# Gate and up projections of a feed-forward as seven-product block products

## The reference

```python
    Wg = dequant_nvfp4(gate_W_packed, gate_scales)   # (4096, 512)
    Wu = dequant_nvfp4(up_W_packed, up_scales)       # (4096, 512)
    Wd = dequant_nvfp4(down_W_packed, down_scales)   # (512, 4096)
    gate = jnp.einsum('th,nh->tn', xt, Wg)
    up = jnp.einsum('th,nh->tn', xt, Wu)
    gelu = jnp.tanh(0.7978845608028654 * (gate + 0.044715 * gate ** 3)) * gate * 0.5 + gate * 0.5
    inter = gelu * up
    out = jnp.einsum('tn,hn->th', inter, Wd)
    ...
x = x + _L0_ffn_ref(_layernorm(x, axis=-1), ...)
```

## Time and profile before

| what | us |
|---|---|
| median of 3 runs (1642.74 to 1647.78) | 1646.12 |
| the profiled execution's own time | 1646.68 |
| its span, first to last instruction | 1644.9 |
| TensorE busy in the span | 1526.4 (93%) |
| VectorE busy | 893.8 (54%) |
| ScalarE busy | 560.6 (34%) |
| GpSimd busy | 123.2 (7%) |

### The profile page before, as it was taken

How to read it: one execution, slowest core, us unless ns; L and a number is a source line. 1 busy time by engine, 2 the same in 40 slices (tenths; PEclk the granted TensorE clock), 3 DMA queues, 4 the chain that set the end, 5 groups by cost and what they waited for, 6 DMA issues and landing times.

```text
span 1644.9 us, 29227 instructions
## 1 busy us (share of the span) xinstructions
PE 1526.4 (93%) x9280; PEld 769.8 (47%) x9280; DVE 893.8 (54%) x2152; ACT 560.6 (34%) x1323; POOL 123.2 (7%) x189
## 2 busy tenths in 40 slices
PE   5887987897899788999999999999999999999998
PEld 3355445544554554444444444444444444444443
DVE  7488468567855976555434534534534544444222
ACT  4378148526833862221212222221222222222111
POOL 1512002100200352000000000000000000000000
PEclk8979989998999999999999999999999999999999
DMA  6641432142125221212112112112112111111111
GB/s 192 163 141 52 122 92 66 59 128 89 60 65 155 88 86 38 81 41 80 40 40 80 40 40 79 41 40 75 45 40 72 48 40 65 54 40 43 59 51 51
DMA packets 73553, 118.41 MB, mean 72 GB/s; under 512 B 10096, under 2 KB 54384, under 8 KB 68848
## 3 DMA queue, kind: packets, MB, share of 16 engines
q1 hardware_dynamic: 73456, 117.20, 22.7%
HBM read 93.32 MB, written 23.86 MB: 71 GB/s over the span
## 4 chain that ended last, share of the span: by engine, by line
PE 79%; DVE 10%; issue 6%; DMA 2%; SPq 1%; ACT 1%; DVEq 0%; ACTq 0%
PE bank L534 23%; PE bank L536 23%; PE bank L535 23%; DVE bank L1135 3%; PE bank L591 3%; PE bank L610 2%; PE bank L547 1%; DVE mx L1135 1%; PE bank L580 1%; DMA qk_dram<-qk 1%; DVE w_split L1328 1%; PE bank L619 1%; DVE prob_t L1149 1%; DVE nmx L1142 1%; PE bank L664 1%
## 5 line engine op out<-in xcount | busy, mean ns | idle before, releaser
L534 PE MATMUL bank<-xf,ring 128*128 128x512 f16 x1024 | 388.1, 379 | 0.0
L535 PE MATMUL bank<-xf,ring 128*128 128x512 f16 x1024 | 388.1, 379 | 0.0
L536 PE MATMUL bank<-xf,ring 128*128 128x512 f16 x1024 | 388.1, 379 | 0.0
L1258 DVE SCALAR_TENSOR_TENSOR inter<-bank,col,gel 128x512 f32<-128x512 f32 x128 | 96.0, 750 | 377.9 <-PE bank L536 377.6
L534 PE MATMUL bank<-ring,hid 128*128 (+1 forms) x512 | 194.1, 379 | 4.2 <-DVE o_t L1122 1.8
L964 ACT CAST hid<-inter 128x512 f16<-128x512 f32 x128 | 79.3, 619 | 347.8 <-DVE inter L1258 331.9
L535 PE MATMUL bank<-ring,hid 128*128 (+1 forms) x512 | 194.0, 379 | 0.0
L536 PE MATMUL bank<-ring,hid 128*128 (+1 forms) x512 | 194.0, 379 | 0.0
L960 ACT ACTIVATE gel<-bank,col 128x512 f32<-128x512 f32 x128 | 88.0, 688 | 300.5 <-PE bank L536 300.5
L591 PE MATMUL bank<-ident,prob 128*128 128x128 f32 x640 | 122.4, 299 | 44.4 <-DVE prob_t L1149 37.8
L1135 DVE CUSTOM_DVE_ANT_0 bank<-bank,mask,col 128x128 f32<-128x128 f32 (+3 forms) x256 | 142.5, 557 | 38.3 <-PE bank L580 24.5
(11 more groups left out here) (141 smaller groups left out, 1820.0 us busy)
## 6 DMA issues: line engine op xcount, KB each, us to landing
xf<-xf_dram SPq DMA_DIRECT2D x32, 1024.0 KB, 4.9
stack<-qk_dram SPq DMA_DIRECT2D x128, 128.0 KB, 3.2
sc_in<-scale_t SPq DMA_DIRECT2D x32, 384.0 KB
qk_dram<-qk SPq DMA_DIRECT2D x32, 256.0 KB, 3.1
packed_t<-pk_t SPq DMA_DIRECT2D x32, 192.0 KB, 2.0
pk_in<-packed_t SPq DMA_DIRECT2D x32, 192.0 KB
X<-in_x_dram SPq DMA_DIRECT2D x4, 1024.0 KB, 6.9
pk_in<-L_ffn_gate_W_packed_dram SPq DMA_DIRECT2D x16, 256.0 KB, 2.9
```

What stands on the lines that cost most here:

```text
L534: pe.matmul(o, lhs(0), rhs(0), start=first, stop=False)
L535: pe.matmul(o, lhs(0), rhs(1), start=False, stop=False)
L536: return pe.matmul(o, lhs(1), rhs(0), start=False, stop=stop)
L1258: nc.vector.scalar_tensor_tensor(inter[:, q], bank[2 * q + 1][:], C_I, gel[:, q], ALU.mult, ALU.mult).then_inc(int_out, 1)
```

## The change

The four batches are taken as two pairs. For a pair, the activations are a two by two block matrix: its two contraction blocks are the two nibbles' rows (each of two tiles of 128), its two column blocks the two batches (512 columns each). The weights of a block of 256 hidden rows are a two by two block matrix too: two blocks of 128 hidden rows by the same two contraction blocks. Their product, eight block products before, is made from seven block products of sums of blocks (Strassen's, in Winograd's form). It is done for gate (x = 0) and for up (x = 1).

- TensorE: `product` makes one of seven block products, two contraction tiles by three matmuls, into banks 0 to 3; three of the seven are added onto what a bank holds. `group` runs the new order: for each pair of batches, two blocks of 256 hidden rows (q = 0, 1) with 2 x 7 products each, and then `down` for the two batches, 48 matmuls each. This is called a pass below: 168 + 96 matmuls, 16 passes. The first block of a pass is q = 0.
- VectorE: `first_sums` and `corners`, four sums of a bank and an SBUF tile for each of gate and up; `inner`, the product of gelu and up, from SBUF but for one; `hidden_tail`.
- ScalarE: `copy_x`, `copy_z`, two copies out of a bank for each of gate and up; `gelu`; `hidden_head`; `heads`, the heads of the weights in three or four pieces.
- GpSimd: `corner`, one sum for each of gate and up, and `weight_sum`, four sums of weight blocks per half block. Heads and tails are now made of the weights' sums too.
- The sums of activation blocks are made once for each pair (`operand_part`, 13 steps for each of two halves, one half on VectorE and one on GpSimd), and both pairs stay in SBUF. The loads of xf at each iteration go.
- In the attention of the last batch GpSimd does more of the first blocks' weights (`weights_beside`). The output is stored tile by tile.

```diff
+        PRODUCTS = ((A11, B11, 0), (S2, T2, 1), (S3, T3, 3), (S1, T1, 2), (A12, B21, 0), (A22, T4, 3), (S4, B22, 2))
...
+            if step in (5, 8, 11, 12):
+                eng.wait_ge(t_hi[h], 4 * pair + (5, 8, 11, 12).index(step) + 1)
+            out, in0, in1, op = ((t1, x(B12, 0), x(B11, 0), ALU.subtract), (t1, t1, x(B12, 1), ALU.add), (t1, t1, x(B11, 1), ALU.subtract),
...
+            ops.tensor_tensor(out, in0, in1, op).then_inc(t_step[h], 1)
...
-            def mlp_loads(i2, odd, dequant, nxt):
...
+            for d in range(2 * NB - B, 2 * NB):
+                b = d % B
+                for t in range(TT):
+                    sp.wait_ge(acc_out, TT * d + t + 1)
+                    sp.dma_start(out[b, P * t:P * t + P, :], X[:, b * TT + t, :]).then_inc(out_stored, 16)
...
+            def corner(m, x):
+
+                pool.wait_ge(comb, 8 * m + 4 * x + 2)
+                pool.wait_ge(c_copied, 4 * m + 2 * x + 2)
+                nc.gpsimd.tensor_tensor(c22[x][:], c22[x][:], m5[x][:], ALU.add).then_inc(c22_out, 1)
...
+            def closing():
+                for step in range(4, T_STEPS):
+                    operand_part(pool, nc.gpsimd, 0, 1, step)
+                for which in (0, 1, 2, 3):
+                    tail(0, 1, which)
+                corner(0, 0)
...
-            def gate_up(it, par, s):
...
+                elif which == IN_C11:
+                    pe.wait_ge(c_copied, 4 * m + 2 * x + 1)
+                elif which == IN_C21:
+                    pe.wait_ge(comb, 8 * m + 4 * x + 2)
...
+                for h in range(2):
+                    mm = three(bank[at][:], lambda a: G[slot][:, op_w, a, 2 * x + h, :], lambda a: xs[pair][:, op_x, a, h, :],
+                               h == 0 and which < IN_C11, h == 1, which >= IN_C11)
+                mm.then_inc(prod, 1)
...
+            def gate_up(m, w, q, weights):
+                copy_x(m, 0)
+                copy_z(m, 0)
+                gelu(m, 0)
+                gelu(m, 1)
+                gelu(m, 2)
+                copy_x(m, 1)
+                gelu(m, 3)
+                copy_z(m, 1)
+                for idx in range(4):
+                    hidden_head(m, w, q, idx)
+                if weights is not None:
+                    heads(*weights)
...
+            def first_sums(m, x):
+
+                dve.wait_ge(prod, product_done(m, x, IN_Y))
+                dve.wait_ge(c_copied, 4 * m + 2 * x + 1)
+                nc.vector.tensor_tensor(c12[x][:], bank[1][:], c21[x][:], ALU.add).then_inc(comb, 1)
...
+            def hidden(m, q):
+                inner(m, 0)
+                corners(m, 1)
+                hidden_tail(m, q, 0)
+                inner(m, 1)
+                inner(m, 2)
+                hidden_tail(m, q, 1)
+                inner(m, 3)
+                hidden_tail(m, q, 2)
+                hidden_tail(m, q, 3)
...
+            def gate_up(m, q, early, weights, late):
+
+                first_sums(m, 0)
+                if early is not None:
+                    tails(*early)
+                if weights is not None:
+                    unpack(*weights, range(0, 3))
+                corners(m, 0)
+                if weights is not None:
+                    unpack(*weights, range(3, 6))
+                first_sums(m, 1)
+                if weights is not None:
+                    scaled(*weights)
+                hidden(m, q)
+                if late is not None:
+                    tails(*late)
...
+            def closing(n):
+                for step in range(T_STEPS):
+                    operand_part(dve, nc.vector, 0, 0, step)
+                residual(n, wo_full, 4, C_O, x1_done)
+                norm_beside(1, n, 0, True)
```

More of the change, by code:

```diff
@@ new lines, in weight_sums, with head, tail @@
+            def weight_sums(nb, half):
+                for which in range(4):
+                    weight_sum(nb, half, which)
+            def head(nb, half, which):
+                weights_whole(pool, nb, half, which)
+                dst, src = piece(nb % 3, half, which, 0)
+                nc.gpsimd.tensor_copy(dst, src).then_inc(dq_hi, 1)
+            def tail(nb, half, which, ops=None):
+                pool.wait_ge(dq_hi, 7 * nb + 3 * half + which + 1)
+                (lo, full), hi = piece(nb % 3, half, which, 1), piece(nb % 3, half, which, 0)[0]
+                if ops is not None:
+                    lo, full, hi = lo[:, ops], full[:, ops], hi[:, ops]
+                ins = nc.gpsimd.tensor_tensor(lo, full, hi, ALU.subtract)
+                done = low_sem(half, which)
+                if done is not None and (ops is None or ops.stop == 4):
@@ new lines, in products, with down @@
+            def products(m, x, which, pair, slot, nb):
+                for one in which:
+                    product(m, x, one, pair, slot, nb)
+            def down(w, pair, beta, slots, nbs):
+                d = 2 * w + beta
+                first = isinstance(d, int) and d == 0
+                if first:
+                    pe.wait_ge(spread_lo[2], B * KT)
+                pe.wait_ge(wd_lo, nbs[0] + 1)
+                pe.wait_ge(hid_lo, 8 * w + 2 * beta + 2)
+                for r in range(2):
+                    for t in range(TT):
+                        if r == 0 and not first:
+                            pe.wait_ge(acc_out, 4 * d + (t - 3))
+                        three(bank[4 + t][:], lambda a: hid[:, beta, 0, r, a, P * t:P * t + P], lambda a: Wd[slots[0]][:, a, r, :], r == 0, False)
+                pe.wait_ge(wd_lo, nbs[1] + 1)
+                pe.wait_ge(hid_lo, 8 * w + 2 * beta + 6)
+                for t in range(TT):
+                    for r in range(2):
+                        mm = three(bank[4 + t][:], lambda a: hid[:, beta, 1, r, a, P * t:P * t + P], lambda a: Wd[slots[1]][:, a, r, :], False, r == 1)
+                    mm.then_inc(down_done, 1)
```

736 lines of the change are left out of this document (473 added, 263 removed).

## The result

| | median us | lowest to highest | runs |
|---|---|---|---|
| before | 1646.95 | 1642.74 to 1649.22 | 6 |
| after | 1635.86 | 1633.23 to 1641.61 | 6 |

The ratio is 0.9941, with a 95% interval of 0.9921 to 0.9962: the changed kernel is faster by 0.6%. The forecast was 1626, inside a range of 1598 to 1648. The sign and the range hold; 20 us of gain were forecast and 11 came.

The account below looks back on a forecast made before the run. TensorE's matmuls, 0.2155 us each, were taken to bound the kernel. 1646.7 - 82.8 (matmuls removed) + 61.8 (more TensorE idle time) - 3.5 (tail) + 4 (attention) = 1626 us, range 1598 to 1648.

Parts of the forecast that it names:

- The clock: Rival for the feed-forward's start: a fall to 1.2 GHz for 20 us or more, 10 us or more added; chance 0.04.
- the attention: Last batch's attention: GpSimd's added ops hold up den_all and similar small ops, 4 us more, bounds 0 and 9.
- the port: VectorE ops with two SBUF inputs and GpSimd's exclude each other for whole instructions, about 1.86 us for a step of each.
- late loads: Four operand loads, 2 MB, issued near 583 and landed at about 593; being late could cost 0 to 2 us.
- the start and pass 1: TensorE waits from the last output projection on: 23 us at the feed-forward's start, 8 us in pass 1.
- the tail: End of the run: last store in quarters, 3.9 us from TensorE's end for 7.5, 3.5 us less.
- the middle terms: Output projection to pass 2, forecast 172.9 us, and pass 2 to the last matmul's start, forecast 836.6 us.
- The products removed: Gate/up matmuls in the feed-forward: 2688 for 3072, 384 fewer at 0.2155 us, 82.8 us less.
- The place that is late: Hand-over between a pass's two blocks: TensorE waits 2.3 us for ScalarE's copy, queued behind four weight heads.
- The two small waits: In each pass, TensorE waits 0.2 us for a sum and 0.6 us for the hidden tile before the first down stage.
- Rival 2: VectorE and GpSimd seldom hold each other up: TensorE idles 41.6 us in place of 71.5, end 1592; chance 0.09.
- Rival 1: VectorE's added ops are dearer; gate products from two SBUF inputs at half speed give 1665; chance 0.14 with its like.

Follow-up runs that it names:

- e2: The changed kernel with ScalarE's four weight heads moved behind the copy of the next block's first product: 1597.86 us, ratio 0.9704.
- e1: The changed kernel with SP issuing the four operand loads at the start of the third quarter's turn, ahead of the packed-weight stores: 1628.86 us, ratio 0.9902.
- e3: The changed kernel with GpSimd's corner and weight sums cut to one column from the third weight block and third product block on: 1630.96 us, ratio 0.9912.
- e4: The changed kernel with GpSimd's work at the feed-forward's start (nine operand sums, second weight block) cut to one column: 1623.57 us, ratio 0.9867.
- e6: The changed kernel with only the widest of four weight heads (1024 elements) moved behind the next block's copy: 1611.30 us, ratio 0.9790.

## Why the prediction was right in sign and 10 us off in size

Two steps failed. The clock was put at nothing and took 17 us; the attention was put at 4 us for the port and took 8.6, some 7 of it for late loads. The waits had been laid out 14 us too long, which hid most of the first.

Against the profiled execution the forecast was 7 us short: 4.6 in the attention, 1.4 in the start and pass 1, 1.2 in the later passes, and 0.7 back in the tail, where the span ended 3.2 us after TensorE for 3.9. The other 2.6 us are the median above that execution: after's six runs spread over 8 us. But the small differences of the middle terms are a balance of two errors, and that they nearly cancel is luck: 1626 + 17 (clock) - 14 (waits) + 4.6 (attention) - 0.7 (tail) + 2.6 = 1635.5, for 1635.9 measured.

- *The products removed.* Right: 82.8 us. 4352 matmuls behind the output projection, and a pass without pauses (e2) takes 57.7 for an ideal 56.9.
- *The place that is late.* Right: "it waits 2.3 us" was 2.0, at that line, once a pass, behind these heads; e2 shows that nothing else is behind it. The two small waits were laid out too long too, so a pass without clock loss is 59.5 for 60.0, 7 us over 14 passes. *The start:* the named waits stand but for one, 24.5 us for 31. The rows give one reason: I had VectorE and GpSimd take 1.86 us for a step of each, whole instructions one after the other; they take 1.53. So they overlap by 0.3, and the two waits for operand sums are 2.0 us for 4.0. The others came out shorter by less, and I have no row for each.
- *Not in the sum: the clock.* This step failed. I wrote "granted clock 1.00 from 720" and kept a fall as a rival with a chance of 0.04, for the start alone. It came there (0.93 from the output projection to pass 2, which is 24 us at the lower level) and in five of 13 hand-overs: 17 us, near the 14 that my waits were too long, which is why the two middle terms look right. Why it was missed: no row of before had a pause of 2 us amid full work, and I had taken the 0.95 of the earlier trace rows as a sign against a fall. It was one. In the trace of before, the clock of a shorter stretch in it, and TensorE's timeline there:

```profile
632.30:635.70 3.40, 2.86 (x14) 2.87 (x15) 2.67 (x6) 1.72 (x4) 0.00 (x0) 0.50 0.02 5
```

```profile
632.84 3.36 PE L547 MATMUL bank<-ident,xn 128*128 128x128 f32 x16 [4.96 <-DVE xn L1109]
```

For 3.4 of the 34 us the clock stood at its lower level, around the end of a pause of 4.96 us, over turns of 128 columns. A mean near 1 over a long stretch can hold a whole fall. What sets it off was narrowed to the pause (2.0: five times in 13; 1.06: never in 13), not settled further.
- *The attention, "I put 4 us".* This step failed in mechanism. I had the 4 for den_all and its like, held up at the port, and the late load as "0 to 2 us, inside the 4". den_all did not grow (it stands below, for 583 in the earlier trace rows); the 8.6 us were mostly the loads. They were issued at 590.20 and not near 583, since they stand in SP's queue behind two stores of packed words, and those went at 589.28 and 589.66. The last of them landed near 600.6 and not 593. I had read the wait that stands ahead of the loads, and not what stands ahead of that wait. e1 moves them and takes 7.0 off, so the port's part is at most the 1.5 to 2.6 us left.

```profile
L1454 DVE SCALAR_TENSOR_TENSOR den_all<-e_zero,den 128x4 f32<-128x4 f32 x12 | 6.7, 561 | 0.0
```

- *The port.* Right that it makes both wait: VectorE's gate product takes 920 ns for 746, and GpSimd's sum in the passes (below) 1552 for 1158. The Trainium skill, "SBUF — State Buffer", section "Who interferes with whom", says that a VectorE instruction with two SBUF inputs contends with a GpSimd instruction that reads SBUF, and e3 and e4 agree with it. It calls the shared ports an exclusive lock. Laid out for whole instructions in turn, as I did, that gives 1.85 us for a pair of sums; a pair takes 1.53, and the measurement decides. Rival 2, 1592 without such waits, is out for the start, where e4 finds 9 us; in the passes the port sets nothing.

```profile
L625 POOL TENSOR_TENSOR c<-c,m 128x512 f32<-128x512 f32 x56 | 86.9, 1552 | 659.3 <-ACT m L1208 539.4 <-DVE c L1566 120.0
```

- *Rival 1, half speed from two SBUF inputs.* Refuted: 746 ns with two SBUF tiles, 749 with a bank. The Trainium skill, "Vector Engine (DVE) Microarchitecture Reference", section "Points that are easy to get wrong", has this form at half throughput; the measurement decides, and at float32 it is not so. The weight sums on GpSimd were worked out at 0.91 and 0.42 us; the small ones are 454 ns, and of the four large ones two are 994 and 995 ns and two, beside VectorE, 1270 and 1346.

## What to carry to other kernels

Where the bounding engine has work taken away, lay out the queue of the engine that frees its banks: a side job of 2 us ahead of such a copy cost 38 us over the run (e2), though VectorE, the busiest of the helpers, was at 71%. For a load, ask not only what it waits for but which waiting instruction stands ahead of it in its queue. Price a pause of TensorE like these (2 us amid full work) above its own length, at the half pace that may follow, and read the clock in stretches as short as the pauses before a term is called right.

## What the hardware showed that I had not expected

- A pause of 2.0 us amid full work was followed by eight matmuls at 1.2 GHz in five of 13 hand-overs and by none in the others, with the same queue each time; in e1 it was the same five, in e4 six, in e3 eight. At 1.06 us (e6) it was none of 13. Nor does the length alone decide: the pause of 3.32 us for the first sums was followed by half pace in after and e1, and not in e2, e3 and e6. What decides which of them fall stays open.
- So halving the pause is worth more than half: a pass is 60.0 us on average after the change, 58.6 in e6 and 57.7 in e2.
- Two-input sums of VectorE and GpSimd beside each other take 1.53 us each and not 0.69 + 1.16 = 1.85 in turn.
